# Cross-attention on one core: scores of two key tiles ahead of the outputs of two, outputs summed in PSUM over a head group

## The reference

```
x = x + cross(layernorm(x), ctx, ctx, wq, wk, wv, bq, bk, bv, wo, bo)   # x: 1 x 512 x 512, ctx: 1 x 8192 x 512
cross:
    q, k, v = project and split in 16 heads of 32
    scores = einsum('bqhd,bkhd->bhqk', q, k) / sqrt(32)
    attn   = softmax(scores, axis=-1)
    ctx    = einsum('bhqk,bkhd->bqhd', attn, v)
    out    = ctx @ wo + bo
x = x + attention(layernorm(x));  x = x + experts(layernorm(x))
```

## Time and profile before

| | before |
|---|---|
| runs, us | 1511.66, 1512.45, 1506.25 (median 1511.66) |
| span of the profiled execution, us | 1510.6 |
| PE, DVE, ACT busy, us | 1444.6, 966.9, 811.0 |
| cross-attention stage, from the first scores to the last totals | 398.5 to 989.5 us |
| mean granted clock of TensorE | 0.975 |

### The profile page before, as it was taken

One profiled execution on the slowest core, in us unless ns is written; L12 is line 12 of the kernel. 1 busy time (PEld: TensorE's weight loads), 2 busy tenths in 40 slices (PEclk: granted clock), 3 DMA queues, 4 the chain that ended last, 5 costly groups with the idle time before them and its releaser, 6 DMA issues. The chain is left out here.

```text
span 1510.6 us, 21218 instructions
## 1 busy us (share of the span) xinstructions
PE 1444.6 (96%) x7952; PEld 910.1 (60%) x7952; DVE 966.9 (64%) x846; ACT 811.0 (54%) x865; POOL 25.9 (2%) x24
## 2 busy tenths in 40 slices
PE   6999999999799999999999999977799999999996
PEld 4888888888433333333333333325688878887884
DVE  7444444443588888888888888865355556555653
ACT  4122122121488888888888888832264445444551
POOL 2000000000300000000000000000000000000000
PEclk9999999999899999999999999998599999999999
DMA  6855455454685555555555555203044544454441
GB/s 199 253 174 207 176 187 201 167 201 161 189 213 115 112 111 111 111 115 118 116 117 116 112 111 111 56 5 110 28 140 156 178 166 164 153 183 163 163 147 57
DMA packets 136180, 214.26 MB, mean 142 GB/s; under 512 B 7624, under 2 KB 40520, under 8 KB 136144
## 3 DMA queue, kind: packets, MB, share of 16 engines
q1 hardware_dynamic: 136144, 213.78, 48.9%
HBM read 159.23 MB, written 51.38 MB: 139 GB/s over the span
## 5 line engine op out<-in xcount | busy, mean ns | idle before, releaser
L659 ACT ACTIVATE at_p<-at_s 128x1024 f32<-128x1024 f32 x512 | 496.8, 1023 | 91.2 <-PE at_s L612 91.0
L679 DVE TENSOR_TENSOR p_sum<-p_sum,at_p 128x2048 f32 (+1 forms) x208 | 476.8, 2292 | 58.4 <-ACT at_p L659 50.9
L612 PEld LDWEIGHTS at_s<-q_stack,at_k 97*128 97x128 f32 x1024 | 172.8, 189 | 249.0 <-ACT at_p L659 162.2
L612 PE MATMUL at_s<-q_stack,at_k 97*128 (+1 forms) x1024 | 311.5, 424 | 7.7 <-PEq L440 7.0
L625 PE MATMUL at_o<-at_p,at_v 128*32 128x512 f32 x2048 | 273.0, 605 | 0.1
L409 ACT ACTIVATE sc_k_hi<-sc_kp,sc_bk 128x512 fp32r<-128x512 f32 x64 | 44.2, 691 | 125.8 <-PE sc_kp L377 125.8
L139 ACT ACTIVATE sc_c_hi<-sc_c 128x2048 fp32r<-128x2048 f32 x16 | 30.7, 1918 | 150.6 <-PE sc_vp L384 137.6
L1267 DVE TENSOR_TENSOR ex_wi_lo<-ei_wi,ex_wi_hi 128x2048 fp32r<-128x2048 f32 x32 | 73.3, 2289 | 51.2 <-ACT ex_wi_hi L1226 51.2
L341 DVE SCALAR_TENSOR_TENSOR sc_k_lo<-sc_kp,sc_bk,sc_k_hi 128x512 fp32r<-128x512 f32 x64 | 48.0, 750 | 89.3 <-ACT sc_k_hi L409 89.2
L349 DVE TENSOR_TENSOR sc_v<-sc_vp,sc_bv 128x512 f32<-128x512 f32 x64 | 44.1, 690 | 88.8 <-PE sc_vp L384 88.8
L1244 ACT ACTIVATE ex_h<-ex_hp,ex_b_cur 128x256 f32<-128x256 f32 x128 | 53.7, 471 | 86.7 <-PE ex_hp L1125 86.2
(11 more groups left out here) (202 smaller groups left out, 1657.6 us busy)
## 6 DMA issues: line engine op xcount, KB each, us to landing
at_k<-k_hi_scratch SPq DMA_DIRECT2D x128, 256.0 KB, 4.7
ei_wi<-w_in SPq DMA_DIRECT2D x32, 1024.0 KB, 7.3
ei_wo<-w_out SPq DMA_DIRECT2D x32, 1024.0 KB, 5.3
sc_c<-ctx_t SPq DMA_DIRECT2D x16, 1024.0 KB, 8.0
k_hi_scratch<-sc_k_hi SPq DMA_DIRECT2D x16, 1024.0 KB, 4.0
k_lo_scratch<-sc_k_lo SPq DMA_DIRECT2D x16, 1024.0 KB, 6.1
at_k<-k_lo_scratch SPq DMA_DIRECT2D x64, 256.0 KB, 4.3
at_v<-v_scratch SPq DMA_DIRECT2D x64, 256.0 KB, 5.0
```

Source lines behind the costliest of these rows:

```text
L612: last = nc.tensor.matmul(s[r][:, a * NQ:(a + 1) * NQ], k[c][:, j, t * P:(t + 1) * P], q_stack[:, bass.ds(it // PER_GROUP * (HG * NQ) + j ...
L659: nc.scalar.activation(p[t % PR][:, pair * 2 * NQ:(pair + 1) * 2 * NQ], s[u % SR][:, :], ACT.Exp, scale=SCALE).then_inc(p_ready[t % PR], 1)
L679: nc.vector.tensor_tensor(sums, sums, p[t % PR][:, :], ALU.add).then_inc(p_summed[t % PR], 1)
```

## The change

In the code of PE, the scores of two key tiles (four halves) now stand together, then the outputs of both. `AHEAD`, the three score buffers and the four buffers `at_p` stay. `at_o` and `at_totals` are opened (`start`) only in a group's first iteration and closed in its last; DVE copies them to `o_acc` and `total_acc` once for each group and no longer adds, and the two fills on POOL are gone. The PE program is written out for each group: first iteration, a loop over the two in the middle, last iteration; so the group's query columns are constants. DVE's program is written out by group too, with a loop over the iterations.

```diff
@@ PE @@
-            def outputs(it, t):
+            def outputs(it, g, opens, closes, t):
                 c, r = t // KT, t % PR
-                if t == 0:
-                    wait_reuse(pe, o_added, it)
-                if t == BY_PE[0]:
-                    wait_reuse(pe, totals_added, it)
+                if opens and t == 0:
+                    wait_reuse(pe, o_added, g)
+                if opens and t == BY_PE[0]:
+                    wait_reuse(pe, totals_added, g)
                 pe.wait_ge(p_ready[r], exped(it, 2 * t + 1))
...
-            def iteration(it, last):
-                for t in range(TILES):
-                    for u in (2 * t + AHEAD, 2 * t + AHEAD + 1):
+            def iteration(it, g, opens, closes):
+                for t in range(0, TILES, 2):
+                    for u in range(2 * t + AHEAD, 2 * t + AHEAD + 4):
                         if u < 2 * TILES:
-                            scores(it, u)
-                        elif not last:
-                            scores(it + 1, u - 2 * TILES)
-                    outputs(it, t)
+                            scores(it, g, u)
+                        elif not closes:
+                            scores(it + 1, g, u - 2 * TILES)
+                        elif g + 1 < NG:
+                            scores(it + 1, g + 1, u - 2 * TILES)
+                    outputs(it, g, opens, closes, t)
+                    outputs(it, g, opens, closes, t + 1)
...
-            rolled(pe, ITERS, iteration)
+            for g in range(NG):
+                iteration(g * PER_GROUP, g, True, False)
+                with pe.Fori(1, PER_GROUP - 1) as i:
+                    iteration(i + g * PER_GROUP, g, False, False)
+                iteration((g + 1) * PER_GROUP - 1, g, False, True)
@@ DVE @@
+                dve.wait_ge(o_done, g + 1)
+                nc.vector.tensor_copy(o_acc[:, g, :], o[:, :]).then_inc(o_added, 1)
+                dve.wait_ge(p_used[BY_PE[-1] % PR], used((g + 1) * PER_GROUP - 1, BY_PE[-1]))
+                nc.vector.tensor_copy(total_acc[:, g, :], totals[:, :]).then_inc(totals_added, 1)
```

More of the change, by code:

```diff
@@ L575, in _ @@
             nc.gpsimd.memset(p_sum[:, HG * NQ:], 0.0).then_inc(zeroed, 1)
[L576 to L579, removed]
         @block.sync
@@ L597, in _, with scores @@
         def _(pe):
-            def scores(it, u):
+            def scores(it, g, u):
                 c, t, pair, r = u // 2 // KT, u // 2 % KT, u % 2, u % SR
@@ L612, in scores @@
                     last = nc.tensor.matmul(s[r][:, a * NQ:(a + 1) * NQ], k[c][:, j, t * P:(t + 1) * P],
-                                            q_stack[:, bass.ds(it // PER_GROUP * (HG * NQ) + j * NQ, NQ)],
+                                            q_stack[:, (g * HG + j) * NQ:(g * HG + j + 1) * NQ],
                                             start=True, stop=True)
                 last.then_inc(s_ready[r], 1)
-            def outputs(it, t):
+            def outputs(it, g, opens, closes, t):
                 c, r = t // KT, t % PR
-                if t == 0:
-                    wait_reuse(pe, o_added, it)
-                if t == BY_PE[0]:
-                    wait_reuse(pe, totals_added, it)
+                if opens and t == 0:
+                    wait_reuse(pe, o_added, g)
+                if opens and t == BY_PE[0]:
+                    wait_reuse(pe, totals_added, g)
                 pe.wait_ge(p_ready[r], exped(it, 2 * t + 1))
@@ L625, in outputs @@
                     last = nc.tensor.matmul(o[j * D:(j + 1) * D, :], v[c][:, t % KT, j * D:(j + 1) * D],
-                                            p[r][:, j * NQ:(j + 1) * NQ], start=(t == 0), stop=(t == TILES - 1))
-                if t == TILES - 1:
+                                            p[r][:, j * NQ:(j + 1) * NQ], start=(opens and t == 0),
+                                            stop=(closes and t == TILES - 1))
+                if closes and t == TILES - 1:
                     last.then_inc(o_done, 1)
@@ L633, in outputs @@
                         last = nc.tensor.matmul(totals[j * D:(j + 1) * D, :], ones[:, :], p[r][:, j * NQ:(j + 1) * NQ],
-                                                start=(t == BY_PE[0]), stop=(t == BY_PE[-1]))
+                                                start=(opens and t == BY_PE[0]), stop=(closes and t == BY_PE[-1]))
                 last.then_inc(p_used[r], 1)
-            def iteration(it, last):
-                for t in range(TILES):
-                    for u in (2 * t + AHEAD, 2 * t + AHEAD + 1):
+            def iteration(it, g, opens, closes):
+                for t in range(0, TILES, 2):
+                    for u in range(2 * t + AHEAD, 2 * t + AHEAD + 4):
                         if u < 2 * TILES:
-                            scores(it, u)
-                        elif not last:
-                            scores(it + 1, u - 2 * TILES)
-                    outputs(it, t)
-            for u in range(AHEAD):
-                scores(0, u)
-            rolled(pe, ITERS, iteration)
+                            scores(it, g, u)
[5 more added lines that the diff above has]
+                    outputs(it, g, opens, closes, t + 1)
+            for u in range(AHEAD):
+                scores(0, 0, u)
+            for g in range(NG):
[3 more added lines that the diff above has]
+                iteration((g + 1) * PER_GROUP - 1, g, False, True)
         @block.scalar
@@ L667, in _, with iteration @@
             dve.wait_ge(first_zeroed, 1)
-            def iteration(it, last):
-                g = it // PER_GROUP
-                sums = p_sum[:, bass.ds(g * (HG * NQ), HG * NQ)]
+            def iteration(it, g):
+                sums = p_sum[:, g * (HG * NQ):(g + 1) * (HG * NQ)]
                 for t in range(TILES):
@@ L679, in iteration @@
                     nc.vector.tensor_tensor(sums, sums, p[t % PR][:, :], ALU.add).then_inc(p_summed[t % PR], 1)
[L680 to L692, removed]
+            for g in range(NG):
+                if g == 0:
+                    iteration(0, 0)
+                    dve.wait_ge(zeroed, 1)
+                with dve.Fori(1 if g == 0 else 0, PER_GROUP) as i:
+                    iteration(i + g * PER_GROUP, g)
+                dve.wait_ge(o_done, g + 1)
+                nc.vector.tensor_copy(o_acc[:, g, :], o[:, :]).then_inc(o_added, 1)
+                dve.wait_ge(p_used[BY_PE[-1] % PR], used((g + 1) * PER_GROUP - 1, BY_PE[-1]))
+                nc.vector.tensor_copy(total_acc[:, g, :], totals[:, :]).then_inc(totals_added, 1)
 def cross_output(nc, ctx, wo, bo, o_acc, p_sum, total_acc, x_sb):
```

## The result

The changed kernel takes 1529.3 us (median of 4 runs, 1527.37 to 1531.69) against 1510.5 us before (median of four runs now, the fourth 1509.29): ratio **1.0131**, 95% interval 1.0108 to 1.0153. It is slower by about 19 us; the forecast was 1525 us, slower by 13.8, with a range of 1512 to 1537.

The account below looks back on a forecast made before the run. PE bounds the attention stage; a pair's wait for ACT makes 4.385 us against 4.24. Sixteen iterations of 37.66 us give 602.6 against 588.7; put on the 1511.7 us median, that forecast 1525 us, range 1512 to 1537.

Parts of the forecast that it names:

- The chain of the prediction: Cross-attention, one pair of tiles: from scores through ACT's exponential back to PE and both outputs, 4.385 us against 4.24 before.
- group start to exponential: From the start of a pair's scores on PE to ACT's exponential of the half scored first: 0.77 us.
- held half: A pair's fourth half waits for the exponential of the half its group scored first; held to 1.84 us, 0.34 of stall.
- restart to outputs: On PE, one half tile of scores after a stop, up to the outputs: 0.66 us.
- two outputs: On PE, the outputs of both tiles of a pair, in a row: 0.885 + 1.00 = 1.885 us.
- The first rival: The exponential never holds PE in the attention stage, which runs at its own pace: 1474 us, faster; chance 0.07.
- The second rival: PE's restart after the wait is cheaper than 0.66 us: 1512 us, no change, or 1518 with part of it; chance 0.17.
- The third: Gaps on PE make the clock fall in a tenth of the stage: some +50 us, 1575 us; chance 0.03.
- Sums over the group and the unrolled program: DVE's fewer additions and PE's longer program in the attention stage: each taken at zero, upper bounds 0.2 and 2.6 us.
- the stop of 0.32 us per iteration: PE's wait at the next iteration's first key tile, put down to a register; now covered, gaining 4.7 us.
- no scores group that stands out: Sign in the profile after: no scores group on PE longer than the others by 0.32 us.
- ACT's idle of 0.7 us: Sign in the profile after: ACT idle about 0.7 us once in four exponentials, instead of 0.18 in two.

Follow-up runs that it names:

- run 3: Changed kernel, but behind the first four tiles ACT computes only half of each exponential (512 of 1024 columns), output not the reference's: 1477.4 us, ratio 0.9786.
- run 1: Kernel before with only PE's order changed to pairs; sums and rolled loops kept: 1532.1 us, ratio 1.014.
- run 2: Changed kernel put back in the order of single tiles; sums over the group and unrolled PE kept: 1510.6 us, ratio 1.0002.
- run 7: Changed kernel with PE and ACT written out and six one-bank score buffers, one head and one 512-column exponential each: 1469.6 us, ratio 0.9734.
- run 6: Changed kernel in the order of single tiles, PE and ACT written out, three score buffers in turn over the stage: 1506.2 us, ratio 0.9973.
- run 4: Changed kernel with PE and ACT written out over 16 iterations, three score buffers in turn over the whole stage: 1521.9 us, ratio 1.0085.

## Why the prediction was right, and where it was not

**The direction and its cause.** The chain of the prediction is the measured one. Its terms: group start to exponential 0.77 (989.18 to 989.95), held half at 1.85 (1.84 forecast), restart to outputs 0.66 (0.66), two outputs 1.855 (1.885). A pair takes 4.365 us, where the forecast had 4.385 and PE alone 3.94 (run 3). Runs 1 and 2 put the whole loss on the order of pairs; runs 3 and 7 take the hold away in two ways (a shorter exponential; buffers that come free by the head) and both turn the loss into a gain, 1477 and 1470 us. The first rival's 1474 us is thus near what the order is worth when the chain doesn't bind, as the forecast worked out.

**The second rival** fell: the restart took the full 0.66 us, nothing of it saved. (Its 4.34 us a pair would make 1519 us, not 1518; nothing hangs on that.) **The third** fell: the clock stayed at 1.00 between 440 and 960 us, though PE stood idle 26 of these 520 us. Sums over the group and the unrolled program, taken at zero, can't be told from zero in the time (run 2).

**What was mis-sized: the stop of 0.32 us per iteration.** "The kernel before" says that half u waits for the exponential of u-3; that holds inside an iteration only. The prediction put the stop down to a wait on a register for the next keys, said that it lies ahead of the held half and is covered, and booked a gain of 4.7 us from that. The cause was another. Buffer numbers restart in each iteration, so half 32 waits for half 30, two back instead of three, and half 33 for 31. In the order of before 32 was held for the exponential of 30 (run 2: it stays without the register; run 6: it goes when the buffers are taken in turn). In pairs half 32 isn't held, and the 4.7 us are gained, as was booked: the group at 547.63 has its first four matmuls out in 1.20 us, as any other. But half 33 needs the buffer that the same group has just given to 31: PE is held at the third half instead of the fourth, and the half behind it is late too, 2.98 us instead of 2.51. That is 0.46 us, 15 times, 6.9 us, so the end of an iteration costs 2.2 us more than before where 4.7 less was forecast; run 4 gives back 6.8 in the stage and 7.4 in the time. Of the signs that the prediction named, "no scores group that stands out" therefore did not come: fifteen stand out, by 0.46. I had read `u mod 3` as running on over the iterations; the code of `scores` has a branch for u < 3 that says otherwise, and the place of the stop, always between halves 31 and 32, should have sent me there, and so should the first stop, which the prediction's own "14 x 0.32 + 0.24" counts though no register is there.

**Two smaller terms.** Two outputs were put at 0.885 + 1.00 = 1.885 us, but the earlier trace rows already show outputs, then totals, then scores at 607.21, 608.10 and 609.07, 1.86 us: a second run of the same kind is followed after 0.97, not 1.00. And ACT's idle of 0.7 us counted the last of four exponentials with 0.92, the distance of starts; it lasts 1.02, which gives 0.6, and 0.59 was measured.

**The sum again, with what was measured.** 16 x (8 x 4.365 + 2.58) = 600.0, plus 6.9, is 606.9 against the 588.7 of before: +18.2 where the trace has +17.6. The forecast of +13.8 was short by the 6.9 and long by 0.02 us in each of 128 pairs, 2.6 us. The times differ by 18.8 us; the remaining 1.2 us are within the spread of the runs. The total came a little nearer than its terms, by luck: 6.9 us too few and 2.6 too many.

## What to carry to other kernels

Before work is grouped to save changes of kind on one engine, count for each buffer how many steps back its last user is, and how many of those steps fall into the same group: a buffer that the group itself has just filled turns another engine's latency (here 0.77 + 1.02 + 0.05 us) into a stop, however much capacity that engine has left. Freeing buffers in smaller pieces cured it in the same memory. And where a ring of buffers restarts in a loop whose length it doesn't divide, look at the seam on its own: the distance is shorter there, and a small stop at a fixed place of the loop is its sign.

## What was not expected of the hardware

- Two outputs in a row take 1.86 us up to the next scores (544.08 to 545.94 in run 4), where 1.885 was expected. Why the second is 0.03 us shorter than one that stands alone stays open.
- An exponential of 512 columns costs ACT 0.50 us from start to start, one of 1024 columns 0.92: halving it adds only 0.04 us to each half, and one takes less than the 0.55 us of the expectation's bad case. In run 7 that is 512 x 0.08 = 41 us more of ACT's time, all beside PE's work.
